# Rows of ones from GpSimd instead of VectorE, and twelve stack loads at twelve tiles in a row

## What is computed

```
x = x + 0.5 * ffn(layernorm(x))      # 8 experts, top 2, 176 hidden
x = x + attn(layernorm(x))           # 16 heads of 16, rope, causal softmax
x = x + 0.5 * ffn(layernorm(x))
```

## Time and profile before

| | |
|---|---|
| median of three runs | 1312.65 us |
| profiled execution | 1310.62 us |
| its span | 1308.9 us |
| TensorE busy | 1066.9 us, 82% |
| VectorE busy | 910.0 us, 70% |
| ScalarE busy | 632.4 us, 48% |
| GpSimd busy | 601.4 us, 46% |
| DMA, mean | 90 GB/s |
| projection | about 308 to 468 us |
| attention | from 468 us |

### The profile page before, as it was taken

One profiled execution on the slowest core, in us unless ns is written; L12 is line 12 of the kernel. 1 busy time (PEld: TensorE's weight loads), 2 busy tenths in 40 slices (PEclk: granted clock), 3 DMA queues, 4 the chain that ended last, 5 costly groups with the idle time before them and its releaser, 6 DMA issues. The chain is left out here.

```text
span 1308.9 us, 24181 instructions
## 1 busy us (share of the span) xinstructions
PE 1066.9 (82%) x6982; PEld 722.4 (55%) x6982; DVE 910.0 (70%) x2809; ACT 632.4 (48%) x1314; POOL 601.4 (46%) x757
## 2 busy tenths in 40 slices
PE   1958998890688659999999999999987788988850
PEld 1957987780576613333333333333286688977740
DVE  5787444444798768988999988898176894444436
ACT  1301555550576604666666666666762204555420
POOL 1923777773699801222222222222306707777750
PEclk9999999995799957999999999999986558999975
DMA  6611333321466531112111111100003402233339
GB/s 215 206 33 39 98 98 98 99 80 44 120 180 181 170 103 52 51 53 62 57 60 59 56 52 57 61 32 2 2 1 116 146 1 89 91 96 95 97 112 326
DMA packets 84077, 117.44 MB, mean 90 GB/s; under 512 B 11358, under 2 KB 64364, under 8 KB 80880
## 3 DMA queue, kind: packets, MB, share of 16 engines
q1 hardware_dynamic: 67200, 79.17, 19.3%
q0 software_dynamic: 13632, 33.59, 8.2%
q10 hardware_dynamic: 3120, 3.15, 0.7%
HBM read 75.48 MB, written 43.78 MB: 91 GB/s over the span
## 5 line engine op out<-in xcount | busy, mean ns | idle before, releaser
L1257 ACT ACTIVATE a_probs<-a_ps_s 128x1024 f32<-128x1024 f32 (+3 forms) x384 | 294.3, 813 | 173.1 <-PE a_ps_s L1289 171.9
L1172 POOL TENSOR_SCALAR_AFFINE_SELECT a_probs<-a_probs 128x256 f32<-128x256 f32 x256 | 102.5, 406 | 369.6 <-ACT a_probs L1257 366.9
L1190 DVE CUSTOM_DVE_ANT_0 a_unused<-a_ps_m,const_sb 128x128 bf16<-128x128 f32 (+3 forms) x512 | 234.1, 485 | 26.7 <-PE a_ps_m L1274 16.8
L1274 PE MATMUL a_ps_m<-st_k,st_q 96*128 96x512 bf16 (+3 forms) x768 | 219.7, 345 | 24.4 <-PEq L155 17.1
L354 POOL DMA_INDIRECT v_sb<-xn_dram,f_token_i x142 | 145.4, 1024 | 124.0 <-issue 80.5
L1192 DVE TENSOR_REDUCE a_max_a<-a_ps_m 128x1 f32<-128x512 f32 x256 | 175.7, 686 | 14.3 <-PE a_ps_m L1274 13.9
L1289 PE MATMUL a_ps_s<-st_q,st_k 98*128 98x512 bf16 (+3 forms) x768 | 180.8, 329 | 1.5 <-ACT a_probs L1257 1.4
L1274 PEld LDWEIGHTS a_ps_m<-st_k,st_q 96*128 96x128 bf16 x768 | 67.9, 98 | 196.6 <-DVE a_max_a L1192 55.9
L476 DVE TENSOR_TENSOR f_h<-f_ps_gu,f_sg 128x176 f32<-128x176 f32 x142 | 48.5, 341 | 175.3 <-ACT f_sg L537 175.3
L1302 PE MATMUL a_ps_ctx<-a_probs,a_v_st 128*32 128x512 f32 (+3 forms) x1536 | 163.7, 498 | 1.3 <-POOL a_probs L1172 0.6
L359 POOL DMA_INDIRECT y_dram<-v_sb,f_pair_i x142 | 143.5, 1011 | 43.5 <-issue 41.0
(11 more groups left out here) (172 smaller groups left out, 2249.3 us busy)
## 6 DMA issues: line engine op xcount, KB each, us to landing
xn_dram<-v_sb SPq DMA_DIRECT2D x64, 128.0 KB, 3.4
p_yb<-y_dram SPq DMA_DIRECT2D x32, 256.0 KB, 2.8
v_sb<-y_dram SPq DMA_DIRECT2D x32, 256.0 KB, 3.8
st_q<-qk_dram SPq DMA_DIRECT2D x16, 384.0 KB
st_k<-qk_dram SPq DMA_DIRECT2D x16, 384.0 KB
qk_dram<-st_rT_hi SPq DMA_DIRECT2D x16, 256.0 KB, 2.9
qk_dram<-st_rT_mid SPq DMA_DIRECT2D x16, 256.0 KB, 3.5
qk_dram<-st_rT_lo SPq DMA_DIRECT2D x16, 256.0 KB, 5.1
```

What stands on the lines that cost most here:

```text
L1172: pool.affine_select(out=tri, in_=tri, compare_op=ALU.is_ge, fill=zero, base=0, pattern=[[0, 2], [1, P]], channel_multiplier=-1).then_inc( ...
L1190: dve.tensor_tensor_reduce(unused[:, bank, 0:nk], ps, cst("mask")[:, HALF - nk:HALF], 1.0, NEG, ALU.add, ALU.max, at).then_inc(taken, 1)
L1257: act.activation(probs[:, s % 4, :, 0:nq], ps_s[s % 2][:, :, 0:nq], ACT.Exp, scale=float(HD) ** -0.5).then_inc(exp_done, 1)
L1274: pe.matmul(ps_m[bank][:, 0:nk], q_st[b][0:MAX_ROW, h, P * i:P * i + P], k_st[b][0:MAX_ROW, h, k0:k0 + nk], start=True, stop=True).then_in ...
```

## The change

The four memsets move from the start of VectorE's queue in the projection to GpSimd's queue in attention, behind the first copy of v, and GpSimd waits for its own memsets there. TensorE no longer waits for them before the first pass of group 0; it waits at the start of each group's second pass, for as many memsets as there are groups so far, at most four. SyncE issues the twelve stack loads one at each tile from 14 to 25, each behind the store of that tile, and none after the last store.

```diff
-    def fill(self, dve):
+    def fill(self, pool):
         for k in self.k:
-            dve.memset(k[MAX_ROW:ROWS, :, :].rearrange("p h s -> p (h s)"), 1.0).then_inc(self.filled, 1)
+            pool.memset(k[MAX_ROW:ROWS, :, :].rearrange("p h s -> p (h s)"), 1.0).then_inc(self.filled, 1)
...
-                if t >= 14 and t % 2 == 0:
-                    load_stacks((t - 14) // 2)
+                if 0 <= t - 14 < 4 * len(RUNS):
+                    load_stacks(t - 14)
...
             store(NT // 2 - 1)
-            load_stacks(4 * len(RUNS) - 1)
...
-            stacks.fill(dve)
             moments_of = Moments(dve, stats_own, stats, mv, x_sb, rstd, nmr)
...
             copy_v(0, 0)
             zero = pool.to_reg(0.0)
+            pool.wait_ge(v_copied, 1)
+            stacks.fill(pool)
+            pool.wait_ge(stacks.filled, RING)
...
-            pe.wait_ge(stacks.filled, RING)
             pe.wait_ge(stack_in[0], LOADS)
...
                     if s == 0:
-
+                        pe.wait_ge(stacks.filled, min(g + 1, RING))
                         pe.wait_ge(max_in[b], turns(g, b) * 32)
```

## The result

Over seven runs each, beside one another, the changed kernel took 1305.46 us (1303.02 to 1307.51) and the kernel before 1313.36 us (1310.78 to 1316.44). The ratio is 0.9938, with a 95% interval of 0.9923 to 0.9953: 0.6% faster, 8 us. The prediction was 1305 us, on the median's footing 1307. The profiled execution has a span of 1304.3 us, 4.6 us under that of before: it took 1306.03 us, 0.6 us more than the median of its kernel, and that of before 1310.62 us, 2.7 us less than the median of its own.

What follows compares the result with a forecast made beforehand. VectorE was taken to bound the projection, with two DMA engines carrying the heavy stack loads nearly as tight. -9.0 us at attention's start, +2.4 (clock) and +1.1 (short count) gave -5.5 us: 1310.6 to 1305 us, range 1293 to 1315.

Steps and rivals of the forecast that it cites:

- Memsets off VectorE: Projection start: VectorE's first mix moves from 325.65 to 312.4 us, and everything behind it with it, -13.2 us.
- SyncE's load 0: Projection: the first stack load is issued at 375.9 us instead of 389.05 us.
- 64.6 us of work on the hot engines: Tiles 14 to 25: two DMA engines, taken to carry all 384 and 256 KB loads, delay pair 10's stores to 442.5 us.
- the short count: Projection: the count of DMA work put a y landing 1.1 us too early, so 1.1 us was added.
- From there to GpSimd's last low part 14.2 us: Projection end, after ScalarE's tile 26 high part: 18.43 us before, less a 4.23 us store wait.
- 2.4 us for two tiles at a lower clock: Projection: long stalls leave TensorE at a lower clock; two that no DMA wait hides add 2.4 us.
- Tail 1.5 + 1.0 us: Projection end: last three stores issue undisturbed in 1.5 us, then 1.0 us from SyncE's last issue to attention.
- GpSimd's fill costs nothing: Attention start: four GpSimd memsets, 4.9 us each, end before the first select; cost would start at 8.5 us each.
- A DMA share without the dips of before: Projection, 376 to 443 us: a sign that the forecast is right, beside several ScalarE waits of 3 us and more.
- the first (DMA engines don't bind): Projection: y loads and stores slip past the stack loads, giving 1290.3 us; chance 0.16.
- The second (384 KB loads hold their engines longer, 8 us): Projection: 8 us per 384 KB load beside other traffic, four add 11.6 us, giving 1316.7 us; chance 0.12.
- The third (all of the gain lost): Projection: SyncE's in-order issues meet a full queue, 0.8 us lost per pair, 5 us more, 1310 us; chance 0.17.

Runs made afterwards that it cites:

- the fill alone: Only the memsets of ones move to GpSimd, stack loads stay at every second tile, against the kernel before: ratio 0.9882, and 0.9894 when run again.
- the profiles with more loads: Changed kernel with two third-stack loads issued at tile 16 instead of in attention: ratio to the kernel before 1.0036 (384 KB loads), 1.0018 (256 KB loads).
- 16-row loads: Changed kernel with each two- or three-block stack load split into 16-row loads: ratio to the kernel before 0.9799; with two other load schedules 0.9789 and 0.9790.
- the kernel with more GpSimd memsets: Changed kernel with 18 more GpSimd memsets, into a tile nobody reads, behind the ones and before the first select: ratio to the kernel before 1.0035.
- the loads alone: Only the stack loads move, to every tile from 14 to 25, memsets stay on VectorE, against the kernel before: ratio 1.0026, slower by 3.6 us.

## Why the prediction was right, step by step

- **Memsets off VectorE, -13.2 us.** The first mix was predicted near 312.5 us and came at 311.76, the phase having begun 0.7 us earlier. The mechanism is shown by the fill alone.
- **SyncE's load 0 at 375.9 us**: 375.17 us.
- **64.6 us of work on the hot engines, the stores of pair 10 landed at 442.5 us, 1.1 us more by the short count**: 443.28 us, and 441.68 us in the second profile. The total was right; whether each term was is not shown. If a 384 KB load costs the 6.6 us of the profiles with more loads, not 5.1, that is 6 us more over four of them, and others must have been counted some 6 us too high: the stores of 2.8 us, perhaps, or the start. If it costs the 5.6 us of their times, it is 2 us. The terms for stores and y loads were never measured beside heavy loads, so the right sum may owe something to luck.
- **From there to GpSimd's last low part 14.2 us, and 2.4 us for two tiles at a lower clock**: 459.93 - 443.28 = 16.65 us against 16.6, 16.1 us in the second profile. Here luck can be seen. With 16-row loads the same stretch (481.25 - 465.98) has no DMA wait, and the full clock until 476 us, and takes 15.3 us, so the 14.2 us were 1.1 us too short: not all of the 4.23 us taken off had been lost time. What is left for the clock is at most 1.4 and 0.8 us, not 2.4. The price of 1.2 us a stall was read wrongly, too: it sets a tile with mixing (3.94 us) against one without (2.74 us), where a steady tile with mixing takes 3.3 us. Two errors of 1 us and a little more met. Two stretches of the full change behind the stall, and one of the kernel with 16-row loads, with its high part of tile 26 and its last low part:

```profile
443.00:446.00 3.00, 1.02 (x3) 0.62 (x4) 1.48 (x3) 2.72 (x7) 1.16 (x1) 0.50 0.22 61
446.00:449.00 3.00, 3.00 (x10) 2.52 (x10) 1.92 (x5) 0.71 (x2) 1.93 (x2) 0.50 0.65 174
469.00:472.00 3.00, 3.00 (x20) 2.67 (x19) 2.55 (x7) 2.02 (x5) 2.63 (x3) 1.00 0.52 144
465.98 0.60 ACT L992 ACTIVATE st_rT_hi<-p_ps_rT 128x512 bf16<-128x512 f32 x1
478.99 2.26 POOL L893 TENSOR_TENSOR st_rT_lo<-p_rT_rest,st_rT_mid 128x512 bf16<-128x512 f32 x2 [0.42 <-ACT st_rT_mid L996]
```

  The granted clock of 0.50 is the 1.2 GHz level. In the 7 us before it TensorE was busy for 3.26 us. In the stretches with the earlier stalls it is 0.93, 0.68 and 0.84, and 1.00 before them.
- **Tail 1.5 + 1.0 us**: SyncE is through at 461.52 us, attention begins at 462.52 us. With all additions the prediction had 462.7 us. Its sign "first matmul near 459 us" left the additions out.
- **GpSimd's fill costs nothing**: confirmed, with 20.1 us of cover in front of the select. A memset took 3.51 us, not the 4.9 us taken from the copy.
- **A DMA share without the dips of before**: this sign didn't come. The share is 0.60, 0.52, 0.53 and, from 416 to 443 us, 0.47, in the mean lower than before. The waits came all the same, so the mean share was not a sign of the hot engines being busy.
- **The two halves apart** were predicted less well than their sum, if the length of the projection is the measure: -13.2 and +7.7 us; measured on one chip -11.4 us for the fill, and +4.7 us for the loads behind it (149.1 to 153.8 us, the latter in the kernel with more GpSimd memsets, which don't touch the projection), or +6.1 to +6.9 us without the fill. By the time of the whole kernel they are -14.7 or -16.4 us and +3.6 us.

Of the rivals, the first (DMA engines don't bind) falls with the loads alone. The second (384 KB loads hold their engines longer, 8 us) falls in its size: 5.6 to 6.6 us, around the 6.5 us named as its turning point, and the time didn't turn. Whether they are longer at all stays open. The third (all of the gain lost) falls, though its mechanism is there: store issues of 4 to 7 us, more than the 2.24 us that it went by.

What stays open: the measured gain, 8 us (6 to 10), is larger than the 4.9 and 6.9 us by which the projections of the two profiles of the full change are shorter than before's, and the same holds for the other kernels: 16.4 and 14.7 us against 9 to 11 for the fill alone, 27.9 against 26 with 16-row loads, +3.6 against +6 to 7 for the loads alone. One part is known, the 3.3 us that the profiles of before and after lie closer together than the medians. The rest of the kernel shows no mechanism: from the copy of v to the first select there is 0.06 us between them, and from the first select to the last it is 445.0 us before, 447.3 and 445.5 us in the two profiles of the full change. The projection begins anywhere from 342.4 to 349.5 us on the two chips where the kernel before takes 1385 us and more, with the same code ahead of it.

The kernel that beats both is the one with 16-row loads, at 0.979 to 0.980 of before, three times the gain of the change, by splitting loads alone once the fill is off VectorE.

## What to carry to other kernels

Ask how many engines a transfer uses, and don't stop at the mean DMA share: here two- and three-part loads, taken to be on two and three engines, made the y loads and stores behind them wait at a share of 0.5. Count the work of the busiest engine up to each wait; when a schedule is made denser, that count, and not the tail it removes, says what happens. Before loads are moved in time, try to split them into loads of 16 rows; here the schedule then no longer mattered. And set profiles beside medians: the length of one phase in one profile was uncertain by 2 us here, a quarter of the gain.

## What the runs showed of the hardware

- A DMA issue can hold SyncE for long while heavy loads are in the queue: 7.07 us in the full change for one store, which takes 0.57 us undisturbed. That the queue is full then is inferred.
- A memset of 2 x 4096 bf16 takes GpSimd 3.51 us and VectorE 3.47 us, but VectorE has 0.80 us between two of them and GpSimd none: four take 13.86 us on GpSimd and 16.3 us on VectorE. One of 128 x 2048 bf16 takes GpSimd 33.46 / 18 = 1.86 us. In these two shapes the time went by the elements of a partition, not by the number of partitions.
- In the kernel with a stretch at a DMA share of 1.02 and 237 GB/s y loads landed after 5.6 us at most, in the full change, with 0.52 and 155 GB/s, after up to 12.9 us.
- Two chips differ by 5.5% on the same kernel, all of it ahead of the projection and in the second mixture: the projection began at 308.4 and 343.8 us and took 159.8 and 160.6 us; from the copy of v to the second mixture it was 525.0 and 525.3 us, and from there to the end 315.7 and 353.7 us.
